# Edge marks written before the edge counts, edge maxima beside the projections, and four heads gathered in BF16 halves

## The chip, the cores and the metric

One Trainium2 chip, of which the kernel uses one core. The time is the device time of one launch in microseconds (us). Three runs of the kernel before gave 1710.49, 1711.12 and 1711.81 us: the median is 1711.12. A further execution was profiled, and all rows below come from it.

## The reference

A graph transformer layer on 1250 nodes of 768 features with 21250 edges. The layer norm of `x` feeds a graph attention network (GNN, three layers of four heads of 192 channels on the same 21250 edges) and a linear-attention mixing (12 heads of 64, 256 random features); both are added to `x`. After a second norm comes a mixture of 8 experts.

```python
def gat_conv(x, src, dst, W, a_src, a_dst, b):        # for each of the 3 layers, N=1250, H=4, C=192
    h = (x @ W).reshape(N, H, C)
    e = leaky_relu(((h * a_src).sum(-1))[src] + ((h * a_dst).sum(-1))[dst], 0.2)
    m = segment_max(e, dst, N)
    p = exp(e - m[dst])
    s = segment_sum(p, dst, N)
    out = segment_sum((p / (s[dst] + 1e-16))[:, :, None] * h[src], dst, N)
    return out.reshape(N, H * C) + b
x1 = relu(xn @ W_ah + b_ah)                           # xn = layernorm(x)
node = relu(concat([relu(gat_conv(x1, ...)) for 3 layers], 1) @ W_out + b_out)
# mixing: q, k, v = xn @ w_qkv.T
# q' = ratio * (exp(q.proj - diag - max over features) + eps), k' likewise with one maximum over all keys
# mix = (q' @ (k'.T @ v)) / (q' @ sum k') @ w_proj.T + b_proj
x = x + node + mix
x = x + ffn(layernorm(x))                             # top-1 switch to 8 experts, capacity 195
```

## The kernel before

The edges are turned into a dense table of counts: `count[s, d]` says how often edge s to d occurs (1250 x 1250). With it a GAT head is dense work: the weight of a pair is exp(leaky_relu(as[s] + ad[d]) - shift[d]) times its count, and the sum over edges is a matrix product of these weights with `h`. A head has ten *items*: half of the destinations (640 or 610) by a pair of source tiles (2 x 128). Twelve heads make 120 items. The nodes lie in 10 tiles of 128 (the last has 98), so `NT` is 10.

One item goes through four steps. `edge_z` on DVE (`L1538`, two instructions) adds the source term to the shifted destination rows `shift_b`; `edge_exp` on ACT (`L1931`, two) is the exponential; `weigh` on DVE (`L1547`, one of 1280 columns) takes the minimum with 1 and multiplies by the counts; `gather` on PE (`L1085`, ten FP32 matmuls of 193 columns, each shown as two by the trace) multiplies with the rows `hb`. Five buffers `eb` hold weights. After a half head, `evict` (ACT) and `finish` divide and store.

The shifts need, for each head and destination, the largest source term among its edges. `edge_max` on DVE (`L1503`) takes it over 1250 sources for one tile of destinations: 120 instructions. Its other operand, `absent`, is 0 at an edge and a very large negative number elsewhere; `shifts` then makes the head's shift, and SP writes it to memory and reads it back spread over the partitions (`shift_b`, in `head_in`).

How the counts come about: GpSimd (POOL) fills three tables in device memory with zeros (`table<-zero`), then adds 170 groups of 125 edges into them with indirect DMAs (`L2142`, `table<-amount,place`), each table's adds waiting for the last ones into the same table. `tab_in` reads ten tiles of each table back, DVE's `count_` sums the three, ACT copies to BF16 (`count16`), PE transposes them (`count_turn`, 100 of 128x128), and DVE makes `absent` of the transposed tile.

All engines follow one order of steps, written by generators (`whole_order`), and each engine runs its own steps of it in that order, held back only by semaphores. `first_order` holds the norm, `x1` = relu(...), and `h` of three layers. Then two streams are laced together: `projection_steps` (v products, `L912` and neighbours; q and k products of six pairs of heads; `k_top`, the maxima of the keys, whose banks `L1028` reuses) followed by `mix_steps`, and beside it `graph_steps`. In `mix_steps` each pair of heads has ten k steps (`dash`, `L1102`; `k_sum`, `L1117`) and ten q steps (`q_max`, `L1570`; `q_turn`; `q_out`, `L1145`, for two tiles), and then the rows: `row_turn` (`L1160`), `row_mm` (output products of 18 matmuls of 384 columns), 10 row tiles for the mixing and 10 for each GNN layer. A GNN layer's row tiles wait for that layer's 40 gathers. `graph_steps` waits for the count adds to be in (`COUNTS_AT`, q/k product 17), then does counts and `absent`, then edge maxima, then items. The rates (`COUNT_RATE`, `EDGE_RATE` and others) say how many steps of the second stream go by one of the first. In `features`, `warm_mix` issues two idle matmuls of 512 columns on PE with each step until the items are open.

After the rows comes the tail: norm, switch, experts, with the indirect reads `L2162` of 105 or 90 rows on POOL.

## Time and profile before

| what | value |
|---|---|
| runs | 1710.49, 1711.12, 1711.81 us |
| profiled execution | 1709.37 us, its span 1707.6 us |
| mean granted TensorE clock | 0.962 |
| busy share of the span | PE 90%, weight load 70%, DVE 67%, ACT 40%, POOL 24% |
| stages: norm, x1, h | to 311 us |
| v products; q and k products | 314 to 377; 377 to 571 |
| mixing without items; mixing with items | 571 to 646; 646 to 972 |
| items and row products | 972 to 1387 |
| last row products; tail | 1387 to 1431.5; 1431.5 to 1707.6 |

The span runs from the first to the last instruction, and the execution is 1.77 us longer. Row products of the first tile start at 1013.6 us. The page's 40 slices, of 42.7 us each:

```profile
PE   3989999999878789998999989998999999986987
PEld 2556666555444568988888988888888976656664
DVE  6677664105567989999987787668766833885323
ACT  3420001122233366877777763346434621441110
POOL 3688888888500000000000000000000000002331
PEclk9989999999989899999999999999999999986999
```

Each digit is a tenth of the slice (9 is 90% or more). POOL is busy with the count adds to slice 11. DVE is nearly idle in slice 8, where the v products run, and nearly full in slices 14 to 22, where edge maxima, mixing and items come together. PE is at 9 in nearly every slice after 30: from there on it is PE that is short.

### The profile page before, as it was taken

What the parts mean: (1) busy time and instruction counts of PE and PEld (TensorE: products, weight loads), DVE (VectorE), ACT (ScalarE), POOL (GpSimd) and SP (SyncE); (2) the same over time, 40 slices, a digit from 0 to 9 for tenths busy, and PEclk for the clock granted to TensorE, in tenths of its full rate; (3) what the DMA queues carried; (4) which work ended last, traced back from release to release, by engine and by line L of the source; (5) the groups of instructions that cost most, each with busy time, mean ns of one, the idle gap of its engine ahead of it and who ended that gap; (6) DMA issues with size and microseconds to landing.
All of it is one profiled execution on the core that took longest, in us unless ns stands there. A gap on an engine that the chain in (4) does not pass through costs nothing.

```text
span 1707.6 us, 25848 instructions
## 1 busy us (share of the span) xinstructions
PE 1541.5 (90%) x10083; PEld 1186.8 (70%) x10109; DVE 1149.2 (67%) x2629; ACT 681.4 (40%) x1359; POOL 410.1 (24%) x251
## 2 busy tenths in 40 slices
PE   3989999999878789998999989998999999986987
PEld 2556666555444568988888988888888976656664
DVE  6677664105567989999987787668766833885323
ACT  3420001122233366877777763346434621441110
POOL 3688888888500000000000000000000000002331
PEclk9989999999989899999999999999999999986999
DMA  9435545464752514324420354236413224545951
GB/s 342 97 64 113 111 84 122 71 93 75 190 187 87 143 42 120 88 90 114 125 71 28 104 166 162 96 126 197 129 38 103 82 68 153 213 181 203 319 158 50
DMA packets 196620, 213.72 MB, mean 125 GB/s; under 512 B 81551, under 2 KB 149789, under 8 KB 196498
## 3 DMA queue, kind: packets, MB, share of 16 engines
q1 hardware_dynamic: 119874, 187.01, 34.6%
q0 software_dynamic: 75760, 22.70, 8.8%
q10 hardware_dynamic: 864, 2.36, 0.4%
q8 instruction: 80, 1.31, 0.3%
q14 instruction: 42, 0.34, 0.1%
HBM read 144.74 MB, written 68.40 MB: 125 GB/s over the span
## 4 chain that ended last, share of the span: by engine, by line
PE 45%; DVE 19%; POOL 17%; DMA 9%; issue 7%; ACT 3%; SPq 1%; POOLq 0%; ACTq 0%; DVEq 0%
PE bank L1085 17%; POOL table L2142 17%; DVE junk L1503 5%; PE bank L913 4%; PE bank L911 4%; PE bank L912 4%; PE bank L1261 4%; DMA table<-amount,place 3%; PE bank L1249 3%; DVE eb L1538 2%; DVE eb L1547 2%; PE bank L1145 2%; DMA table<-zero 2%; PE bank L1117 1%; PE bank L1102 1%
## 5 line engine op out<-in xcount | busy, mean ns | idle before, releaser
L1085 PE MATMUL bank<-hb,eb 128*128 128x193 f32 (+3 forms) x2400 | 418.8, 332 | 14.5 <-ACT node L1945 9.2
L1085 PEld LDWEIGHTS bank<-hb,eb 128*128 128x128 f32 (+3 forms) x2400 | 399.5, 191 | 20.6 <-issue 10.5
L2142 POOL DMA_INDIRECT table<-amount,place x170 | 345.2, 2030 | 74.4 <-issue 49.1
L2148 POOL IOTA iota8i<- 128x8 int32 x1 | 0.1, 140 | 941.7 <-DMA node_rows<-node 941.7
L1538 DVE SCALAR_TENSOR_TENSOR eb<-shift_b,as_low,shift_b 128x640 f32<-128x640 f32 (+1 forms) x240 | 196.4, 860 | 0.3 <-PE bank L1085 0.2
L1931 ACT ACTIVATE eb<-eb,asd 128x640 f32<-128x640 f32 (+1 forms) x240 | 181.5, 812 | 28.9 <-DVE eb L1538 28.9
L1547 DVE SCALAR_TENSOR_TENSOR eb<-eb,count 128x1280 f32<-128x1280 f32 (+1 forms) x120 | 174.6, 1455 | 2.3 <-ACT eb L1931 2.3
L1503 DVE CUSTOM_DVE_ANT_0 junk<-ab,absent 128x1250 bf16<-128x1250 f32 x120 | 174.3, 1453 | 1.5
L911 PE MATMUL bank<-w_o_hi,aT_hi 128*128 128x384 bf16 (+1 forms) x360 | 119.1, 331 | 0.0
L911 PE MATMUL bank<-wg_hi,x1T_hi 128*128 128x384 bf16 (+3 forms) x360 | 118.9, 330 | 0.1
L913 PE MATMUL bank<-w_o_hi,aT_lo 128*128 128x384 bf16 (+1 forms) x360 | 119.0, 330 | 0.0
L912 PE MATMUL bank<-w_o_lo,aT_hi 128*128 128x384 bf16 (+1 forms) x360 | 118.9, 330 | 0.0
L912 PE MATMUL bank<-wg_lo,x1T_hi 128*128 128x384 bf16 (+3 forms) x360 | 118.8, 330 | 0.0
L913 PE MATMUL bank<-wg_hi,x1T_lo 128*128 128x384 bf16 (+3 forms) x360 | 118.8, 330 | 0.0
L912 PE MATMUL bank<-xnT_lo,wq_hi 128*128 128x512 bf16 (+1 forms) x212 | 74.9, 353 | 4.6 <-DVE wq_lo L1339 3.0
L1377 DVE TENSOR_TENSOR h_row<-bank,bgr 128x384 f32<-128x384 f32 (+1 forms) x60 | 32.5, 555 | 64.8 <-PE bank L913 64.7
L913 PE MATMUL bank<-xnT_hi,wq_lo 128*128 128x512 bf16 (+1 forms) x215 | 75.8, 352 | 0.2
L1803 DVE TENSOR_TENSOR orow<-bank,b2r 105x384 f32<-105x384 f32 (+1 forms) x32 | 17.8, 555 | 82.8 <-PE bank L1261 82.8
L1970 ACT ACTIVATE ef<-bank,q_shift 128x256 f32<-128x256 f32 (+1 forms) x120 | 50.5, 473 | 51.2 <-DVE q_shift L1575 51.0
L911 PE MATMUL bank<-xnT_hi,wq_hi 128*128 128x512 bf16 (+1 forms) x201 | 70.8, 352 | 0.1
L1877 ACT ACTIVATE wg_hi<-stage 128x776 bf16<-128x776 f32 x18 | 15.3, 850 | 135.5 <-DVE stage L1353 135.5
L1945 ACT ACTIVATE node<-bank 128x386 f32<-128x386 f32 (+1 forms) x72 | 29.3, 442 | 88.3 <-PE bank L1085 88.3
(280 smaller groups left out, 2965.9 us busy)
## 6 DMA issues: line engine op xcount, KB each, us to landing
w<-in_w SPq DMA_DIRECT2D x16, 1152.0 KB, 12.5
shift_b<-shift_rows SPq DMA_DIRECT2D x24, 625.0 KB, 5.8
h_rows<-h_row SPq DMA_DIRECT2D x27, 388.0 KB
hb<-h_rows SPq DMA_DIRECT2D x12, 873.0 KB
ar<-node_rows SPq DMA_DIRECT2D x27, 384.0 KB
table<-zero POOLq DMA_DIRECT2D x3, 3054.0 KB, 21.7
tab<-table SPq DMA_DIRECT2D x27, 312.5 KB, 3.6
qk_rows<-qk_row SPq DMA_DIRECT2D x12, 625.0 KB
```

The costliest lines, as they stand in the source:

```text
L911: T.matmul(out_ap, lhs[0], rhs[0], start=first, stop=False, skip_group_check=skip)
L912: T.matmul(out_ap, lhs[0], rhs[1], start=False, stop=False, skip_group_check=skip)
L913: return T.matmul(out_ap, lhs[1], rhs[0], start=False, stop=last, skip_group_check=skip)
L1085: ins = T.matmul(bank[w // 2][0:M, c0:c0 + GC + 1], p[0:K, u, w * P:w * P + M], hv[0:K, t, 0:GC + 1], start=opens and u == 0 and w % 2 == ...
L1249: ins = T.matmul(bank[i % 2][:, 0:CAP], w1s[e % WEIGHT_SETS][:, k, f * 128:(f + 1) * 128], sT_of(k)[:, e * CAP:(e + 1) * CAP], start=k == ...
L1261: ins = T.matmul(bank[4 + i % 4][0:r1 - r0, 0:HROWS], hT[e % 2][:, f, r0:r1], w2s[e % WEIGHT_SETS][:, f, cs], start=f == 0, stop=f == KF - 1)
L1503: V.tensor_tensor_reduce(out=junk[0:R, :], in0=ab[lh % 2][0:R, :], in1=absent[0:R, t, :], scale=1.0, scalar=-BIG, op0=ALU.add, op1=ALU.max ...
L1538: ins = V.scalar_tensor_tensor(eb[i % EDGE_BUFFERS][:, u, 0:w], low, as_low[:, t, lh:lh + 1], high, ALU.add, ALU.max)
L1547: V.scalar_tensor_tensor(e, e, 1.0, count[:, 2 * pair:2 * pair + 2, ns], ALU.min, ALU.mult).then_inc(sem["edge_w"], 1)
L1931: ins = A.activation(e[:, u, 0:w], e[:, u, 0:w], ACT.Exp, bias=asd[:, t, 8 * l + hh:8 * l + hh + 1])
L1970: ins = A.activation(ef[g % 4][0:R, hh, :], bank[3 + g % 2][0:R, hh * FEATS:(hh + 1) * FEATS], ACT.Exp, bias=bias)
L2142: G.indirect_dma_start(tables[i], bass.IndirectOffsetOnAxis(place[:, c:c + 1], axis=0), amount16[:, c:c + 1], None, compute_op=ALU.add).th ...
```

## The change

**Marks.** Three new tables in device memory, `marks`, in BF16, are filled with the large negative number, and 0 is written at each edge, at the transposed place, and at the whole diagonal (one DMA of 1250 elements). These 170 indirect DMAs write and don't add (`L2191`). They stand on POOL where the 170 adds stood. SP reads ten tiles of each into `absent` and two `tab` buffers (`absent_in`), and DVE takes the maximum of the three (two instructions a tile, `absent_`). `count_turn` and `count16` are gone.

**Counts.** The 170 adds stand on POOL behind the marks (`scatter`), and `tab_in` stands behind them, on POOL too and no longer on SP. The zero fills of the three count tables stand among the marks, at groups 4, 5 and 6 of `place`. In the order, counts come at step 78 of the mixing (`COUNTS_AT`), the first items behind them.

**Edge maxima.** Five stand beside the v products, 30 beside the q and k products, two at the maximum of the keys, then 0.9 for each mixing step; 107 stand ahead of `tab_in` and 13 behind it.

**Halves.** For heads 8 to 11 (the third layer, items 80 to 119) `h` is stored as two BF16 halves in the room of one FP32 number, and the weights are split in place: their high half is the upper 16 bits, and `weigh_lo` on DVE (`L1419`, 1280 columns) writes the rest, rounded, into the lower. `gather` is then 30 BF16 matmuls of 193 columns for ten FP32 ones. Both operands have a stride of two elements. In `h` of that layer ACT writes the high halves and DVE the low ones.

**Order.** `warm_mix` is gone from the mixing steps. The rates change. The last mixing step stands beside item 39 (before: 48), the first GNN row tile beside item 51 (54), row tile 10 beside item 99 (85), row tile 20 behind all items (112).

```diff
-COUNTS_AT = 17
-COUNT_RATE, EARLY_EDGE_RATE, FIRST_EDGE_RATE, EDGE_RATE, ATTENTION_RATE = 0.5, 0.75, 1.1, (1.1, 0.5), (0.4, 0.5)
+MARKS_AT, COUNTS_AT = 6, 78
+COUNT_RATE, VALUE_EDGE_RATE, KEY_EDGE_RATE, MIX_EDGE_RATE, ATTENTION_RATE = 1.0, 1.8, 0.4, 0.9, (0.8, 0.77)
+SPLIT_FROM = 8
...
     yield from paced((key_steps(), 1), (tiles, 1), (first_nodes(), 1))
+    for q in range(PIECES):
+        yield "scatter", q
...
 def graph_steps(done):
-    while "scattered" not in done:
+    yield "ab_in", 0
+    for _ in range(MARKS_AT):
         yield None
-    yield "ab_in", 0
-    yield from paced((in_step([(3, lambda t: [("count_turn", t), ("absent", t)]), (1, lambda t: [("count", t)]),
-                               (0, lambda t: [("tab_in", t)])], NT), COUNT_RATE))
+    yield from in_step([(1, lambda t: [("absent", t)]), (0, lambda t: [("absent_in", t)])], NT)
     edges = edge_steps(done)
...
+    while "counts" not in done:
+        yield None
+    yield from paced((in_step([(1, lambda t: [("count", t)]), (0, lambda t: [("tab_in", t)])], NT), COUNT_RATE))
     yield "head_in", 0
...
-        if "open" not in done:
-            yield "warm_mix", 2
+        if n == COUNTS_AT:
+            done.add("counts")
...
@@ gather, PE @@
+                        for n, (p_part, h_part) in enumerate(((0, 0), (0, 1), (1, 0))):
+                            ins = T.matmul(bank[w // 2][0:M, c0:c0 + GC + 1],
+                                           eb_parts[i % EDGE_BUFFERS][p_part][0:K, u, w * P:w * P + M],
+                                           hb_parts[lh % 2][h_part][0:K, t, 0:GC + 1], start=begins and n == 0,
+                                           stop=ends and u == 1 and n == 2, skip_group_check=True)
@@ absent_, DVE @@
+                V.tensor_tensor(absent[0:R, t, :], absent[0:R, t, :], others[0], ALU.max).then_inc(sem["absent_first"], 1)
+                ve.wait_ge("absent_first", t + 1)
+                V.tensor_tensor(absent[0:R, t, :], absent[0:R, t, :], others[1], ALU.max).then_inc(sem["absent_done"], 1)
@@ weigh_lo, DVE @@
+                ve.wait_ge("weighed", i - ITEMS * SPLIT_FROM + 1)
+                V.tensor_tensor(low, eb[i % EDGE_BUFFERS][:, :, 0:w], high, ALU.subtract).then_inc(sem["edge_w"], 1)
@@ place_, POOL @@
                 if q == 0:
+                    ge.wait_ge("marks_set", 32)
+                    G.dma_start(marks[2].rearrange("(p t n) o -> p t (n o)", p=P, n=MARKS[1]),
+                                fill[:, :].unsqueeze(1).broadcast_to([P, MARKS[0], MARKS[1]])
+                                ).then_inc(sem["table_zero"], 16)
+                    G.dma_start(marks[0][0:N * (N + 1), :].rearrange("(p r s) o -> p r (s o)", p=EP, s=N + 1)[:, :, 0:1],
+                                none[0:EP, 0:N // EP].unsqueeze(2), allow_slow_non_contiguous=True
+                                ).then_inc(sem["marks_set"], 16)
+                if 4 <= q < 4 + TABLES:
+                    G.dma_start(tables[q - 4].rearrange("(p t n) o -> p t (n o)", p=P, n=TABLE[1]),
...
+                                    [P, TABLE[0], TABLE[1]])).then_inc(sem["table_zero"], 16)
+                ge.wait_ge("placed", 2 * q + 1)
                 for c in range(q * CP, min((q + 1) * CP, CHUNKS)):
                     i = table_of(c)
+                    if i == 0:
+                        ge.wait_ge("marks_set", 48)
                     if i == 2:
+                        ge.wait_ge("table_zero", 16)
+                    ge.wait_ge(f"marked{i}", 16 * added(c, i))
+                    G.indirect_dma_start(marks[i], bass.IndirectOffsetOnAxis(mark_at[:, c:c + 1], axis=0),
+                                         none[0:EP, 0:1], None).then_inc(sem[f"marked{i}"], 16)
@@ tab_in, now POOL @@
+                for i in range(TABLES):
+                    ge.wait_ge(f"scatter{i}", 16 * added(CHUNKS, i))
+                ge.wait_ge("counted", TABLES * (t - 1))
@@ absent_in, SP @@
+                for i in range(TABLES):
+                    sy.wait_ge(f"marked{i}", 16 * added(CHUNKS, i))
+                sy.wait_ge("absent_done", t - 1)
```

POOL's instructions from the marks or adds on, in the kernel before (`L2142` are the adds):

```order
L2122 MEMSET h_row_229 128x4
L2132 DMA table<-zero 1024x1x1527
L2142 DMA table<-amount_72,place 1563648x1 x170
L2148 IOTA iota8i 128x8
L2149 IOTA idx_i 128x10
```

and after (`L2191` the marks, `L2213` the adds, `L2203` the reads of `tab_in`):

```order
L2173 DMA marks<-fill 1024x1x1528
L2176 DMA marks<-zero 1250x1x1
L2191 DMA marks<-zero,mark_at 1564672x1 x32
L2180 DMA table<-zero 1024x1x1527
L2191 DMA marks<-zero,mark_at 1564672x1 x8
L2180 DMA table<-zero 1024x1x1527
L2191 DMA marks<-zero,mark_at 1564672x1 x8
L2180 DMA table<-zero 1024x1x1527
L2191 DMA marks<-zero,mark_at 1564672x1 x122
L2213 DMA table<-amount_72,place 1563648x1 x170
L2203 DMA tab_148<-table 128x1250
```

One chain of adds has become a chain of marks with three fills in it, and the adds and the reads of the tables follow it on the same engine.

DVE among items and the splitting of output weights (`w_o_lo`, `L1590`), in the kernel before:

```order
L1547 SCALAR_TENSOR_TENSOR eb_157<-eb_157,count 128x2x610
L1590 TENSOR_TENSOR w_o_lo<-st_0_242,w_o_hi 128x768
L1590 TENSOR_TENSOR w_o_lo<-st_1_243,w_o_hi 128x768
L1538 SCALAR_TENSOR_TENSOR eb_155<-shift_b_251,as_low,shift_b_250 128x640 x2
L1547 SCALAR_TENSOR_TENSOR eb_153<-eb_153,count 128x1280
L1590 TENSOR_TENSOR w_o_lo<-st_0_242,w_o_hi 128x768
L1590 TENSOR_TENSOR w_o_lo<-st_1_243,w_o_hi 128x768
L1538 SCALAR_TENSOR_TENSOR eb_156<-shift_b_251,as_low,shift_b_250 128x640 x2
L1547 SCALAR_TENSOR_TENSOR eb_154<-eb_154,count 128x1280
```

and after, in the heads in halves (`L1573` is `edge_z`, `L1582` is `weigh`, `L1419` is `weigh_lo`, `L1625` splits output weights):

```order
L1573 SCALAR_TENSOR_TENSOR eb_157<-shift_b_229,as_low,shift_b_228 128x640 x2
L1419 TENSOR_TENSOR eb_160<-eb_160 128x2x610
L1625 TENSOR_TENSOR w_o_lo<-st_1_246,w_o_hi 128x768
L1582 SCALAR_TENSOR_TENSOR eb_156<-eb_156,count 128x1280
L1573 SCALAR_TENSOR_TENSOR eb_158<-shift_b_229,as_low,shift_b_228 128x640 x2
L1419 TENSOR_TENSOR eb_156<-eb_156 128x1280
L1625 TENSOR_TENSOR w_o_lo<-st_0_245,w_o_hi 128x768
L1625 TENSOR_TENSOR w_o_lo<-st_1_246,w_o_hi 128x768
L1582 SCALAR_TENSOR_TENSOR eb_157<-eb_157,count 128x1280
```

Each item has one more instruction of 1280 columns, between its `weigh` and its gather, and up to two splits stand with it as before.

PE at the first steps of the mixing, before (`L1046` are the idle matmuls):

```order
L1046 MATMUL bank<-ident_61 128x512 x2
L1102 MATMUL bank<-feats_hi,k_first 128x256
L1102 MATMUL bank<-feats_lo,k_first 128x256
L1102 MATMUL bank<-feats_hi,k_first 128x256
L1102 MATMUL bank<-feats_lo,k_first 128x256
L1117 MATMUL bank<-v_first,ef_212 128x65 x4
L1046 MATMUL bank<-ident_61 128x512 x2
```

and after (`L1116` is `dash`, `L1131` is `k_sum`):

```order
L1116 MATMUL bank<-feats_hi,k_first 128x256
L1116 MATMUL bank<-feats_lo,k_first 128x256
L1116 MATMUL bank<-feats_hi,k_first 128x256
L1116 MATMUL bank<-feats_lo,k_first 128x256
L1131 MATMUL bank<-v_first,ef_215 128x65 x4
L1116 MATMUL bank<-feats_hi,k_first 128x256
```

The two idle matmuls of each step are gone, and up to the counts nothing stands between the mixing's own matmuls.

## Rows read from the trace of the kernel before

**Rows 1.** Busy time of each engine by stretch of the span; its second row names the columns.
```profile
core 0: us, PE busy (x) PEld busy (x) DVE busy (x) ACT busy (x) POOL busy (x), PEclk, DMA share, GB/s
314.00:377.00 63.00, 60.04 (x362) 36.66 (x362) 2.33 (x11) 11.09 (x22) 54.57 (x28) 0.98 0.51 74
377.00:571.00 194.00, 162.42 (x1327) 92.52 (x1345) 126.24 (x242) 52.72 (x93) 64.84 (x32) 0.93 0.48 127
571.00:646.00 75.00, 65.37 (x433) 48.07 (x432) 67.39 (x128) 47.60 (x105) 0.00 (x0) 0.90 0.43 115
646.00:972.00 326.00, 300.26 (x2205) 287.51 (x2203) 289.01 (x480) 241.56 (x535) 0.00 (x0) 0.98 0.31 88
972.00:1387.00 415.00, 405.23 (x2507) 352.32 (x2506) 300.21 (x394) 191.91 (x346) 0.00 (x0) 0.99 0.37 120
1387.00:1431.50 44.50, 44.50 (x288) 29.36 (x287) 14.82 (x35) 7.84 (x19) 0.96 (x6) 1.00 0.24 72
1431.50:1707.60 276.10, 230.06 (x1338) 166.70 (x1335) 146.30 (x398) 64.60 (x139) 47.64 (x48) 0.91 0.58 193
```

**Rows 2.** Timeline of POOL, indirect adds: start us, busy us, what, [idle before it <-releaser].
```profile
48.80 2.12 POOL L2142 DMA_INDIRECT table<-amount,place  x1 [13.02 <-DMA table<-zero]
...
57.22 1.99 POOL L2142 DMA_INDIRECT table<-amount,place  x1 [3.98 <-DMA table<-amount,place]
...
453.36 1.99 POOL L2142 DMA_INDIRECT table<-amount,place  x1 [0.30 <-issue]
```

**Rows 3.** DMA issues of the page: count, KB each, us from issue to landing.
```profile
shift_b<-shift_rows SPq DMA_DIRECT2D x24, 625.0 KB, 5.8
...
table<-zero POOLq DMA_DIRECT2D x3, 3054.0 KB, 21.7
...
tab<-table SPq DMA_DIRECT2D x27, 312.5 KB, 3.6
```

**Rows 4.** Source view of L2162: ns min/median/max, first and last start.
```profile
L2162 POOL DMA_INDIRECT sr<-xf_rows,from_row x16: 956/986/1542, 1554.7 to 1644.9; - x16
```

**Rows 5.** Timeline of DVE in the mixing, before the first gather.
```profile
602.15 0.69 DVE L1570 TENSOR_REDUCE q_max<-bank 128x2 f32<-128x512 f32 x1
...
604.32 0.69 DVE L1570 TENSOR_REDUCE q_max<-bank 128x2 f32<-128x512 f32 x1
```

**Rows 6.** Timeline of DVE, one item of edge weights and one edge maximum.
```profile
640.41 1.68 DVE L1538 SCALAR_TENSOR_TENSOR eb<-shift_b,as_low,shift_b 128x640 f32<-128x640 f32 x2
642.00 1.48 DVE L1547 SCALAR_TENSOR_TENSOR eb<-eb,count 128x1280 f32<-128x1280 f32 x1
643.40 1.46 DVE L1503 CUSTOM_DVE_ANT_0 junk<-ab,absent 128x1250 bf16<-128x1250 f32 x1
```

**Rows 7.** Groups of instructions by form: xcount, busy us, mean ns of one, idle before.
```profile
L1431 DVE TENSOR_TENSOR sq<-sq 128x512 bf16<-128x512 f32 x24 | 17.6, 735 | 27.6 <-ACT sq L1911 27.6
...
L1339 DVE TENSOR_TENSOR wq_lo<-stage,wq_hi 128x768 bf16<-128x768 f32 x12 | 11.5, 959 | 63.1 <-ACT wq_hi L1867 63.1
```

**Rows 8.** Timeline of PE: mixing, row products, a gather.
```profile
590.29 0.27 PE L1102 MATMUL bank<-feats_hi,k_first 128*128 128x256 bf16 x1
...
590.73 1.01 PE L1117 MATMUL bank<-v_first,ef 128*128 128x65 f32 x8
...
609.67 1.90 PE L1145 MATMUL bank<-context,qf 128*128 128x65 f32 x16
...
1204.15 3.43 PE L1085 MATMUL bank<-hb,eb 128*128 128x193 f32 x20
...
1386.78 0.82 PE L1160 MATMUL bank<-ident,ar 128*128 128x128 f32 x6
...
1399.79 0.82 PE L1160 MATMUL bank<-ident,ar 128*128 128x128 f32 x6
```

**Rows 9.** Waits of PE from 392 to 572 us: us in total, times, longest.
```profile
PE bank L1028 <- DVE kmax L1454: 14.6, 12, 3.8
```

More of the change, by code:

```diff
@@ L238, in product @@
         n, c = divmod(m, NC)
-        if m == COUNTS_AT:
-            done.add("scattered")
+        if m == 0:
+            done.add("products")
         if c == 0 and n + 2 < 2 * PAIRS:
@@ L319, in edge_z, with split_weigh, weigh_last @@
         yield "edge_z", i
+    def split_weigh(i):
+        if i // ITEMS >= SPLIT_FROM:
+            yield "weigh", i
+    def weigh_last(i):
+        yield "weigh_lo" if i // ITEMS >= SPLIT_FROM else "weigh", i
     def of_half(name):
@@ L334, in mark @@
         return []
[L336 to L338 removed]
+    yield from in_step([(5, of_half("finish")), (5, mark), (4, of_half("evict")), (2, split_weigh), (0, edge_z),
+                        (1, lambda i: [("edge_exp", i)]), (2, weigh_last), (3, lambda i: [("gather", i)])],
+                       LH * ITEMS)
     yield "expert_setup", 0
@@ L565, in program @@
         tables = [dram(f"table{i}", (P * TABLE[0] * TABLE[1], 1), U16) for i in range(TABLES)]
+        marks = [dram(f"marks{i}", (P * MARKS[0] * MARKS[1], 1), BF16) for i in range(TABLES)]
         h_rows = dram("h_rows", (LAYERS, N, GH, HW))
@@ L685, in program @@
         tab = [[put(f"tab{i}{j}", [P, N], U16) for j in range(2 + i)] for i in range(2)]
-        count16 = [put(f"count16_{i}", [P, N], BF16) for i in range(2)]
         assert cursor[0] <= r_d
```

195 lines of the change are left out of this document (107 added, 88 removed), and 2 rows, old and new, of the table TAKEN_OVER.

## The prediction, on record before the kernel ran

> **What bounds the kernel now.** I read the table of engines first, then the slices, then the busy time by stretch, and then for each stretch the view that names its limit. In the stretches PE has 162.4 of 194 us beside the q and k products, 300.3 of 326 with mixing and items, 405.2 of 415 with items and row products, 44.5 of 44.5 behind the last gather, while DVE has 2.3 of 63 us beside the v products and 67.4 of 75 in the mixing that has no items yet [rows 1]. So from the first gather at 646 on PE is the limit (with DVE close behind to 972), and ahead of it there is a stretch of 75 us in which DVE makes edge maxima and the mixing must keep step with it. The counts decide when that may begin: POOL adds from 48.8 to 453.36 us, 2.29 us from one to the next where nothing disturbs it (1.99 + 0.30 idle) and 396/167 = 2.37 on the average from 57.22 on [rows 2]. In the waits, PE stands 14.6 us for the key maxima on DVE in the q and k products [rows 9], because DVE has counts, `absent` and the first edge maxima there.
>
> The total of the profiled execution is 1709.37, which is 1.77 above its span and 1.75 below the median of the runs. I work on the span and add both.
>
> **The change part by part.**
>
> *Marks.* The row nearest to an indirect DMA that writes and doesn't add is the tail's: 986 ns, against 1990 ns for an add [rows 2, 4]. With the 0.30 us between, 1.3 us a mark. That row reads 3 KB a line, and a mark writes 2 bytes at 125 places as the adds do, so the two ends are 1.3 and 2.3 us; I take 1.3, since what doubles the add's time is most likely the adding. The first add started at 48.8, when two fills were in [rows 2]; the third marks fill now waits for these, some 9 us, and the diagonal another 3: first mark at 62. 170 x 1.3 = 221, and three zero fills among them hold each the queue behind them for about 9 us (three fills at once take 21.7 to land [rows 3]): 27. Marks are in at about 310. The steps that read them stand at the seventh v product of 20, 314 + 1.5 + 7 x 2.95 = 336. So SP isn't held. `absent` is then 20 maxima of BF16 on DVE, which is idle there.
>
> *Projections.* The v products: 60 of 63 us are PE's own [rows 1]; I add 1.5 for the wait at start: q/k begin at 378. These took 194 us with 162.4 of PE work, of which about 6 are the removed transposes. Left are 156 plus stalls. DVE had 126.2 there; counts and `absent` go (about 27), and 30 edge maxima of 1.5 us replace the fewer of before: about 135 us, under PE's. I put 8 us of stalls in place of 32: 164, ending at 542. Top of the keys to 549.
>
> *Mixing without items.* A q step has a pitch of 2.17 us with one edge maximum [rows 5], a k step a bit less. Of each pair's 20 steps ten cost 2.17 + 0.6 (since 12 maxima come with ten q steps) and ten 1.7: 43.5. Three pairs and ten k steps (17): the engines come to the counts at 549 + 147.5 = 697.
>
> *POOL's chain of adds.* 310 + 170 x 2.37 = 712.5, landing at 715. That is later than 697, so it is POOL that sets the counts. If marks or fills take less, at most 18 us come back. `tab_in` comes on POOL with two buffers: 3.6 us to land [rows 3], three DVE sums of about 0.8 and 0.8 and 0.15 a tile, two tiles per 7.7 us: ten tiles 42, at 757. The head's tables land 5.8 later [rows 3], then `edge_z`, exponential and `weigh`: first gather at **769**, 123 after the 646 of before. Between 549 and 697 nothing is lost by this but place: 70 mixing steps are done that stood beside items before.
>
> *After the first gather.* I sum by the order, taking in each section the engine with the most work. A FP32 gather is 20 passes in 3.27 us, a row product 13.01/4 = 3.25 us, from the two turns at 1386.78 and 1399.79, a k step 0.44 + 0.90, a q step 0.44 + 0.44 + 0.90 (half of the 1.9 for two tiles, less its end) [rows 8].
> 1. Gathers 0 to 38 with 17 k and 20 q steps: 127.5 + 22.8 + 35.6 = 186 us, PE.
> 2. Gathers 39 to 79 with 18 row products: 134 + 58.5, and 3 us where DVE is late: 196 us, PE.
> 3. Gathers 80 to 119, in halves. On PE the same columns in three BF16 passes for two [rows 8]: if each runs at its 193 columns in half of a FP32 pass (0.082 for 0.1635 us), a gather is 2.46 for 3.27, and 40 save 33 us. On DVE an item is `edge_z` 1.59, `weigh` 1.40 to 1.48 [rows 6], and `weigh_lo`. For this, FP32 in and BF16 out, 512 columns take 735 and 768 take 959 ns [rows 7]: 224 per 256 more, so 1280 columns give 1.41 long; with weights of 1220, and a stride of two that no row shows, 1.4. Its ends are 0.85 (at half the rate) and 1.8. So 4.4 us, 4.55 with finish. The first 21 (to item 100) have six splits of output weights (0.9) and two row products beside them: DVE 21 x 4.55 + 5.4 = 101, PE 58: DVE. The last 19 have 14 row products: PE 46.7 + 45.5 = 92, DVE 19 x 4.55 and 14 x 1.3 for row halves = 104: DVE by little. Together 205 us.
> 4. 26 row products without items: 84.5, PE.
>
> The sum is 186 + 196 + 205 + 84.5 = 671.5. The same count of before's order gives 777 from the first gather to row tile 30, and the trace has 1431.5 - 646 = 785.5 [rows 1], 8.5 more. So I add 8: 679.5, 106 less than before. Of these 106, 70 steps of mixing moved ahead, and 33 come from PE's halves, of which DVE takes most back.
>
> *Cut elsewhere.* The 60 idle matmuls (78 less 18; 13 us of PE) lay in time where PE waited, in 571 to 646: nothing by themselves. `h` of layer three costs DVE about 1.1 us a tile more, beside PE's h products, which are longer: nothing. The tail stays 276.1 [rows 1].
>
> Total: 769 + 679.5 + 276.1 = 1724.6 of span; + 1.77 + 1.75 = **1728**; I write 1729 for rounding of the parts. It is 18 us slower than before: 123 late at the first gather against 106 back.
>
> **What a rule says against it.** The row shows FP32 matmuls of 193 columns at 0.1635 us a pass with whole numbers in a row; no row of this stage has a moving operand with gaps. The Trainium skill (SBUF — State Buffer, "Door 1: The DMA port swizzle", the note on cachelines) says that reads lose speed only when fewer than two hits fall in a 16-byte line, and lets BF16 be strided to 8 elements. By that rule a stride of two runs at full rate, as I took; without it rival D would hold.
>
> The granted clock was 0.90 in 571 to 646, with the idle matmuls in it, and 0.98 and 0.99 behind [rows 1]. The Trainium skill (TensorE: Matmul & The Clock Gate, Part 1) has the clock follow how busy the array has lately been. By it the mixing without idle matmuls may fall to the low level of 1.2 GHz; what that would do here is rival C.
>
> **The rivals.**
> - *B, DVE doesn't bind in the halves, and POOL or DVE are ahead elsewhere: faster.* If `weigh_lo` costs 0.85 or less, an item is 3.9 on DVE and section 3 becomes PE's or near it: 205 falls to some 165 (-40). If the zero fills don't hold the marks and the adds keep to 2.29, 15 to 18 us come back at the counts. Both give 1729 - 55 = **1674**. For it: rows of half-width output at 0.87 ns a column [rows 7] are not DVE's quickest form. Against: input is still FP32.
> - *C, the clock falls in the mixing without items.* Between 549 and 697 PE has 1.34 to 1.78 us of work in steps of 1.7 to 2.8, and at 1.2 GHz that becomes 2.7 to 3.6: PE sets the pace, 70 steps x 3.1 = 217 for 147. That ends at 766 for 697, 51 behind POOL's 715, less what one tick of overlap gives back: + 41, **1770**. For it: 0.90 there already [rows 1]. Against: PE stays at more than half of its time.
> - *D, a strided moving operand at half rate.* Each of 1200 BF16 matmuls takes 0.163 instead of 0.082: a gather 4.9, 40 x 4.9 + 52 of row products = 248 for 205, and a few more where both alternate: + 48, **1777**.
> - *E, a mark costs what an add costs.* 62 + 170 x 2.3 + 27 = 480 for the marks, SP stands at `absent_in` from 336 and with it the loads of q and k weights, and the adds end at 885: **1890**. It decides once a mark takes over about 1.45 us (310 would pass 336).
>
> **How the numbers follow.** The forecast has 0.50, B 0.22, C 0.12, D 0.08, E 0.06, something else 0.02. The forecast's own range is 1705 to 1750: 18 us below for POOL's part, 20 above for DVE stalls in the projections. A measurement of this kernel can tell 0.2%, 3.4 us, from no change. Faster: B and a tenth or two of the forecast's own, 0.30; within 0.2%: 0.07; slower: 0.63. The range takes in B and C: 1680 to 1775.
>
> **What would show it.** Right: marks on POOL 1.3 us apart, the last at about 310; the last add at about 712; first gather at about 769; DVE without gaps in gathers 80 to 100 at about 4.5 us an item, PE with gaps there; 30 matmuls of a gather in 2.5 us; row tile 30 at about 1449. Wrong: marks beyond 336 (E); a granted clock near 0.5 between 549 and 769 (C); a gather in halves of 4.9 us (D); or the first gather before 745 with items of 3.9 us (B).

## The result, and the profile after

Four runs of the changed kernel gave 1838.15 to 1846.45 us, median 1839.38, against 1710.8 for the kernel before: a ratio of 1.0765, 95% interval 1.0732 to 1.0799. The forecast was 1729 with a range of 1680 to 1775. The direction was right, the size was not: 129 us slower instead of 18. One execution of the kernel of experiment 7 was disturbed (3077.8 us where the others of that kernel took 1839 to 1848) and is left out of its times.

The profiled execution took 1846.45 us, its span 1844.7. It is the slowest of the four, 7 us above the median, and all rows of the changed kernel come from it. The stretches of the changed kernel, cut at its own events (v products, mixing without items, the gap, items in FP32, items in halves, last row products, tail):

```profile
core 0: us, PE busy (x) PEld busy (x) DVE busy (x) ACT busy (x) POOL busy (x), PEclk, DMA share, GB/s
312.00:407.00 95.00, 65.96 (x364) 38.56 (x364) 15.89 (x31) 8.70 (x19) 66.42 (x47) 0.84 0.58 137
589.00:766.00 177.00, 151.51 (x959) 132.03 (x957) 130.88 (x255) 118.05 (x274) 147.49 (x66) 0.76 0.49 82
766.00:881.00 115.00, 38.98 (x182) 32.88 (x182) 36.66 (x68) 24.06 (x61) 64.83 (x55) 0.52 0.41 106
881.00:1273.00 392.00, 383.77 (x2527) 359.20 (x2526) 313.07 (x430) 239.10 (x470) 0.00 (x0) 0.99 0.35 109
1273.00:1469.00 196.00, 158.56 (x1495) 137.46 (x1493) 191.85 (x210) 92.00 (x163) 0.00 (x0) 0.97 0.31 103
1469.00:1563.00 94.00, 92.11 (x586) 60.40 (x584) 33.83 (x68) 17.88 (x39) 0.96 (x6) 0.98 0.30 88
1563.00:1844.70 281.70, 232.85 (x1338) 168.92 (x1336) 146.41 (x398) 64.77 (x139) 47.55 (x48) 0.91 0.57 189
```

The row that matters is the third: for 115 us PE is busy for 39, DVE for 37, ACT for 24. All of them have come to the counts, and the counts are not there: up to 824 POOL still adds, and from there it reads the tables. The first gather starts at 881.3 instead of 646 [rows 1], 235 us later. Behind it the kernel is quicker than before: 681.8 us to row tile 30, where before took 785.5. The tail has 281.6 for 276.1. 235 - 104 + 5.5 = 137, the difference of the two spans.

What POOL does meanwhile, from its timeline (start, busy us, what, idle before it):

```profile
59.85 1.28 POOL L2191 DMA_INDIRECT marks<-zero,mark_at  x1 [12.68 <-DMA marks<-zero]
...
64.44 1.19 POOL L2191 DMA_INDIRECT marks<-zero,mark_at  x1 [0.30 <-issue]
...
111.26 0.96 POOL L2180 DMA_DIRECT2D table<-zero  x1
...
128.01 1.19 POOL L2191 DMA_INDIRECT marks<-zero,mark_at  x1 [11.11 <-DMA marks<-zero,mark_at]
...
364.88 1.19 POOL L2191 DMA_INDIRECT marks<-zero,mark_at  x1 [0.30 <-issue]
366.38 2.03 POOL L2213 DMA_INDIRECT table<-amount,place  x1 [0.30 <-issue]
...
819.97 1.99 POOL L2213 DMA_INDIRECT table<-amount,place  x1 [0.31 <-issue]
824.23 2.29 POOL L2203 DMA_DIRECT2D tab<-table  x4 [2.27 <-DMA table<-amount,place]
```

From 60 to 824 POOL issues marks, fills and adds, or waits between them. An undisturbed mark takes 1.19 + 0.30 = 1.49 us. Behind each fill a few marks still go out, then POOL waits for one to land: 11.1, 10.7 and 9.4 us. The chain of adds begins when the last mark is out, and `tab_in` when the last add has landed. POOL's groups by form (xcount, busy us, mean ns, idle before them):

```profile
L2213 POOL DMA_INDIRECT table<-amount,place x170 | 372.8, 2193 | 83.1 <-issue 46.0 <-DMA table<-amount,place 37.0
L2191 POOL DMA_INDIRECT marks<-zero,mark_at x170 | 211.1, 1242 | 104.9 <-issue 46.7 <-DMA marks<-zero,mark_at 44.9 <-DMA marks<-zero 12.7
```

The adds of the kernel before:

```profile
L2142 POOL DMA_INDIRECT table<-amount,place x170 | 345.2, 2030 | 74.4 <-issue 49.1 <-DMA table<-zero 13.0 <-DMA table<-amount,place 12.3
```

An add has become longer: 2193 ns on the average for 2030, and the waits for landings are 37.0 us for 12.3. In both kernels the adds are the same 170 instructions.

Last, the halves. DVE's groups by form, and the first two gathers in halves on PE:

```profile
L1573 DVE SCALAR_TENSOR_TENSOR eb<-shift_b,as_low,shift_b 128x640 f32<-128x640 f32 x120 | 100.6, 881 | 5.0 <-PE bank L1093 4.9
...
L1582 DVE SCALAR_TENSOR_TENSOR eb<-eb,count 128x1280 f32<-128x1280 f32 x60 | 89.2, 1487 | 4.4 <-ACT eb L1972 4.4
...
L1419 DVE TENSOR_TENSOR eb<-eb 128x1280 bf16<-128x1280 f32 x20 | 33.5, 1677 | 0.0
L1419 DVE TENSOR_TENSOR eb<-eb 128x1220 bf16<-128x1220 f32 x20 | 31.9, 1596 | 0.1
```

```profile
1273.00 5.39 PE L1097 MATMUL bank<-hb,eb 128*128 128x193 bf16 x60
1278.24 0.32 PE L930 MATMUL bank<-w_o_hi,mix_aT_hi 128*98 128x384 bf16 x1
```

60 BF16 matmuls follow each other in 5.24 us, 0.087 each, against 0.1635 for an FP32 pass [rows 8]. That is 7% above half of it, so the strided operands run near full rate, and rival D (0.163) is out. But `weigh_lo` costs 1.64 us, and in the stretch of the halves DVE is busy for 191.9 of 196 us, PE for 158.6. PE waits there 34.8 us for it:

```profile
PE bank L1097 <- DVE eb L1419: 34.8, 20, 3.0
```

### The profile page after: what moved, and what is told of

The parts are those of the page before. It is cut to its first block, busy times and chain, and to the rows that moved or that the text cites. A ratio compares the mean times of both kernels' runs of the same rounds, so it can differ in the third digit from the quotient of the medians.

```text
span 1844.7 us, 26649 instructions
## 1 busy us (share of the span) xinstructions
PE 1551.1 (84%) x10349; PEld 1187.8 (64%) x10349; DVE 1226.0 (66%) x2705; ACT 683.8 (37%) x1369; POOL 669.9 (36%) x455
## 4 chain that ended last, share of the span: by engine, by line
PE 34%; POOL 23%; DVE 18%; DMA 15%; issue 7%; ACT 2%; SPq 0%; POOLq 0%; DVEq 0%; ACTq 0%
POOL table L2213 16%; PE bank L1093 12%; POOL marks L2191 7%; DMA table<-amount,place 6%; DMA marks<-zero,mark_at 5%; DVE eb L1573 4%; PE bank L930 4%; PE bank L931 4%; PE bank L932 4%; PE bank L1275 3%; DVE eb L1582 3%; PE bank L1263 3%; DVE eb L1419 3%; DMA tab<-table 1%; PE bank L1174 1%
## 5 line engine op out<-in xcount | busy, mean ns | idle before, releaser
L2213 POOL DMA_INDIRECT table<-amount,place x170 | 372.8, 2193 | 83.1 <-issue 46.0
L1093 PE MATMUL bank<-hb,eb 128*128 128x193 f32 (+3 forms) x1600 | 274.7, 329 | 8.0 <-DVE eb L1582 6.0
L1093 PEld LDWEIGHTS bank<-hb,eb 128*128 128x128 f32 (+3 forms) x1600 | 263.3, 189 | 11.1 <-DVE eb L1582 7.2
L2191 POOL DMA_INDIRECT marks<-zero,mark_at x170 | 211.1, 1242 | 104.9 <-issue 46.7
L1573 DVE SCALAR_TENSOR_TENSOR eb<-shift_b,as_low,shift_b 128x640 f32<-128x640 f32 (+1 forms) x240 | 197.3, 866 | 9.3 <-PE bank L1093 9.2
L1582 DVE SCALAR_TENSOR_TENSOR eb<-eb,count 128x1280 f32<-128x1280 f32 (+1 forms) x120 | 174.7, 1455 | 4.4 <-ACT eb L1972 4.4
L1097 PE MATMUL bank<-hb,eb 128*128 128x193 bf16 (+3 forms) x1200 | 115.6, 255 | 37.4 <-DVE eb L1419 34.8
L1097 PEld LDWEIGHTS bank<-hb,eb 128*128 128x128 bf16 (+3 forms) x1200 | 108.1, 102 | 44.9 <-DVE eb L1419 42.0
L1144 PE MATMUL bank<-ident,ef 128*128 128x128 f32 (+1 forms) x240 | 43.6, 313 | 90.9 <-ACT ef L2011 90.6
L1144 PEld LDWEIGHTS bank<-ident,ef 128*128 128x128 f32 (+1 forms) x240 | 31.8, 164 | 100.1 <-ACT ef L2011 99.1
L2233 POOL DMA_INDIRECT sr<-xf_rows,from_row x16 | 16.6, 1034 | 217.7 <-DVE to_row L1812 212.8
```

The lines of the kernel that those rows point to most:

```text
L1093: ins = T.matmul(bank[w // 2][0:M, c0:c0 + GC + 1], p[0:K, u, w * P:w * P + M], hv[0:K, t, 0:GC + 1], start=begins, stop=ends and u == 1, ...
L1097: ins = T.matmul(bank[w // 2][0:M, c0:c0 + GC + 1], eb_parts[i % EDGE_BUFFERS][p_part][0:K, u, w * P:w * P + M], hb_parts[lh % 2][h_part][ ...
L1144: ins = T.transpose(bank[5 + q % 2][:, k * P:k * P + R], ef[g % 4][0:R, hh, m * 128:(m + 1) * 128], ident_of(t))
L1573: ins = V.scalar_tensor_tensor(eb[i % EDGE_BUFFERS][:, u, 0:w], low, as_low[:, t, lh:lh + 1], high, ALU.add, ALU.max)
L1582: V.scalar_tensor_tensor(e, e, 1.0, count[:, 2 * pair:2 * pair + 2, ns], ALU.min, ALU.mult).then_inc(sem["weighed" if lh >= SPLIT_FROM els ...
L2191: G.indirect_dma_start(marks[i], bass.IndirectOffsetOnAxis(mark_at[:, c:c + 1], axis=0), none[0:EP, 0:1], None).then_inc(sem[f"marked{i}"] ...
```

## The experiments

The theory at the start: POOL's chain of 170 marks and 170 adds sets the first gather, and DVE sets the pace in the halves. The rivals: the mixing without items is late by itself (its clock), the halves do save PE's time, and traffic rather than DVE stretches the adds. In each text on record "before" is the unchanged kernel.

### 1. The changed kernel without halves (no_halves)

```diff
-SPLIT_FROM = 8
+SPLIT_FROM = 12
```

> The changed kernel with heads 8 to 11 in FP32 again; everything else stays. The chain theory (POOL's marks and adds set the first gather, DVE sets the pace in the halves): first gather stays near 881 us; items 80 to 119 become PE's, 40 x 3.27 + 16 x 3.25 = 183 us for the 196 of the changed kernel, so about 1826 us (-13). The rival (the halves save PE's 33 us as they stand) expects 196 + 33, about 1872 us.

Measured: 1825.08 us (1820.15 to 1830.10), 14 below the changed kernel. The first gather is at 875.1; items 80 to 119 take 181 us (1267 to 1448) for 196:

```profile
1267.00:1448.00 181.00, 177.14 (x1094) 160.66 (x1093) 134.87 (x170) 90.86 (x160) 0.00 (x0) 1.00 0.34 111
```

PE is busy for 177 of 181 us: the stretch is PE's again, and shorter. The halves cost 14 us in this order. The rival is out. (The text on record counts 16 row products in this stretch; the trace has 14, 84 of the matmuls of one line at six a product.)

### 2. A fifth of the adds (few_adds)

```diff
-MARKS_AT, COUNTS_AT = 6, 78
+MARKS_AT, COUNTS_AT, ADDS = 6, 78, 34
...
@@ tab_in, POOL @@
-                    ge.wait_ge(f"scatter{i}", 16 * added(CHUNKS, i))
+                    ge.wait_ge(f"scatter{i}", 16 * added(ADDS, i))
@@ scatter, POOL @@
-                for c in range(q * CP, min((q + 1) * CP, CHUNKS)):
+                for c in range(q * CP, min((q + 1) * CP, ADDS)):
```

> The changed kernel with 34 of the 170 adds into the count tables; the other 136 are left out, so the counts are incomplete. The chain theory: the last add is at about 460 us, the other engines come to the counts at about 766 as before, first gather about 766 + 57 = 823, so about 1782 us (-58). The rival (the mixing without items and idle matmuls is what is late, at its low clock, and POOL only waits along): first gather stays near 881, 1839 us.

Measured: 1769.09 us (1763.64 to 1775.26), 70 less. The last add is at 458.5 and the engines reach the counts at 755, about as in the changed kernel (765); the first gather is at 805.0. So POOL's chain decides, by 70 us, and no more than that: the other engines come late as well, and the kernel is still 3.6% slower than the one before (ratio 1.0363, 1.0328 to 1.0397).

### 3. Short edge maxima (short_max)

```diff
-MARKS_AT, COUNTS_AT = 6, 78
+MARKS_AT, COUNTS_AT, WD = 6, 78, 50
...
@@ edge_max, DVE @@
-                V.tensor_tensor_reduce(out=junk[0:R, :], in0=ab[lh % 2][0:R, :], in1=absent[0:R, t, :],
+                V.tensor_tensor_reduce(out=junk[0:R, 0:WD], in0=ab[lh % 2][0:R, 0:WD], in1=ab[lh % 2][0:R, 0:WD],
```

> The changed kernel with each edge maximum over 50 columns instead of 1250, so that the maxima are not those of the edges. If DVE's edge maxima are what stretches POOL's adds (2.19 us for 1.99): adds of about 2.03 us, the chain of adds 29 us shorter, about 1810 us. The rival (traffic in the DMA queues holds the adds' landings, and DVE has no part in it): adds stay at 2.19 and the time within 5 us of 1839, since POOL still comes last.

Measured: 1812.09 us (1808.15 to 1815.34), 27 less. POOL's groups in this kernel:

```profile
L2213 POOL DMA_INDIRECT table<-amount,place x170 | 345.0, 2029 | 85.8 <-issue 44.5 <-DMA table<-amount,place 41.3
L2191 POOL DMA_INDIRECT marks<-zero,mark_at x170 | 211.6, 1245 | 99.7 <-issue 44.2 <-DMA marks<-zero,mark_at 40.1 <-DMA marks<-zero 12.3
```

The adds are back at 2029 ns, 170 x 164 ns = 28 us, which is the whole difference; the waits for landings stay (41.3 for 37.0). So both causes are there, and they part cleanly: DVE's edge maxima beside the adds stretch POOL's own instruction, and the landings are held by something else. The mixing's 70 steps change as well:

```profile
577.00:713.00 136.00, 118.98 (x952) 102.57 (x950) 44.44 (x251) 115.73 (x273) 106.86 (x54) 0.96 0.58 105
```

They take 136 us for 176, with DVE busy for 44 of them, and the granted clock is 0.96 for 0.76 though no idle matmul was put back. Experiments 5 and 6 come back to this.

### 4. Only the halves, on the kernel before (halves_only)

The diff is the part of the change on halves, put into the kernel before: `SPLIT_FROM = 8`, the split `h` of layer three, `weigh_lo`, and the three BF16 matmuls.

```diff
+        yield "weigh_lo" if i // ITEMS >= SPLIT_FROM else "weigh", i
```

> The kernel before with only the halves of heads 8 to 11 put in; marks, counts, edge maxima and the order stay as before. The theory that DVE sets the pace in the halves: items 80 to 119 take on DVE 40 x 4.4 + 26 x 1.3 + 11 = 221 us for the 218 of before, so about 1715 us. The rival (PE's 33 us are saved, DVE's addition is hidden): about 1678 us.

Measured: 1706.39 us (1702.39 to 1711.31), ratio 0.9981 (0.9965 to 0.9997). Neither number: nearly nothing is gained, but nothing lost. Items 80 to 119 take 215 us for 218, with DVE busy for 209 of 216, PE for 198. The kernel before, and this one:

```profile
1168.00:1387.00 219.00, 218.61 (x1355) 189.59 (x1356) 152.40 (x203) 99.67 (x182) 0.00 (x0) 0.99 0.30 98
1172.00:1388.00 216.00, 197.52 (x1755) 164.30 (x1756) 208.71 (x243) 100.07 (x183) 0.00 (x0) 0.97 0.31 99
```

So the stretch passes from PE to DVE at nearly no gain: PE's busy time falls by 21 us (by the 0.087 of a matmul, 40 x (3.27 - 2.62) = 26), and DVE gets 40 x 1.64 = 66 more. Here 26 row products stand beside the items, in the changed kernel 14. PE without the halves would need 40 x 3.27 + 26 x 3.25 = 215 here and 176 there, DVE with them was busy for 209 and 192; by these sums the halves cost 14 us there and nothing here.

### 5. A fifth of the marks and of the adds (few_both)

The edit of experiment 2, and:

```diff
@@ place_, POOL @@
-                for c in range(q * CP, min((q + 1) * CP, CHUNKS)):
+                for c in range(q * CP, min((q + 1) * CP, ADDS)):
@@ absent_in, SP @@
-                    sy.wait_ge(f"marked{i}", 16 * added(CHUNKS, i))
+                    sy.wait_ge(f"marked{i}", 16 * added(ADDS, i))
@@ edge_max, DVE @@
-                V.tensor_tensor_reduce(out=junk[0:R, :], in0=ab[lh % 2][0:R, :], in1=absent[0:R, t, :],
+                V.tensor_tensor_reduce(out=junk[0:R, :], in0=ab[lh % 2][0:R, :], in1=ab[lh % 2][0:R, :],
```

> The changed kernel with 34 of 170 marks and 34 of 170 adds, and edge maxima of the same size that read the source terms twice instead of the marks; so marks, counts and shifts are not the reference's. It asks what the order alone is worth once POOL is free. Theory: of the 60 us by which the kernel with few adds is slower than before, 40 come from SP, which stands at the reads of the marks until 360 us: q and k products start at 378 instead of 417, first gather at 765 instead of 805, about 1729 us, still 20 above the kernel before. The rival (the q and k products are late by the reads of the marks themselves, or by the clock): about 1769 us as with few adds.

Measured: 1743.21 us (1739.45 to 1748.31), 26 below few_adds. The q and k products start at 391.0 instead of 417.5, and the first gather is at 784.1. The direction is right. In the changed kernel PE waits here for two things:

```profile
PE bank L930 <- ACT v_row L1947: 28.7, 3, 23.5
PE bank L930 <- DVE wq_lo L1359: 16.0, 1, 16.0
```

The first is for ACT, which empties the banks of the v products into `v_row`, whose buffers SP stores between its reads of the marks; it falls to 0.9 us with few marks. The second, for the split of the first q and k weights, stays at 18.0, and with it 13 us of the delay; in the kernel before it is 3.0. What makes it long was not taken apart. The 70 steps without items take 175 us (559 to 734) though POOL is free:

```profile
559.00:734.00 175.00, 148.53 (x950) 129.92 (x948) 132.98 (x258) 116.89 (x272) 1.59 (x3) 0.77 0.33 88
```

PE is busy for 148.5 us at a mean granted clock of 0.77. That is about half of the time at the low level of 1.2 GHz, and with DVE at 133 of 175 this run doesn't tell which of the two holds the other.

### 6. The same with idle matmuls in the mixing (few_both_warm)

```diff
+        if n < COUNTS_AT:
+            yield "warm_mix", 2
```

> The kernel with few marks and few adds, with two idle matmuls of 512 columns in each mixing step up to the counts, as the kernel before has them. In the 70 steps without items it had PE busy 148.5 of 175 us at a granted clock of 0.77 and DVE 133. If that clock is what makes the mixing long (the clock theory): clock near 0.95, the 70 steps in about 150 us, total about 1720 us. If DVE's edge maxima set the pace: 175 us again, 1743 us.

Measured: 1726.66 us (1725.33 to 1732.30), 17 less. The 70 steps take 159 us (557 to 716), and the clock is up:

```profile
559.00:716.00 157.00, 144.77 (x1098) 113.87 (x1099) 130.57 (x256) 117.64 (x273) 1.59 (x3) 0.99 0.36 94
```

So the idle matmuls that the change took out were worth about 16 us in this stretch once POOL is out of the way. They are not the whole of it: with short edge maxima (experiment 3) the same steps took 136 us at a clock of 0.96 without any idle matmul. So it takes the full maxima on DVE and the missing idle matmuls together to bring the clock down to 0.77. Putting the idle matmuls back gives 16 us of the stretch, shortening the maxima 40, the clock included. In the changed kernel itself that loss lies under POOL's chain: its 70 steps too have a clock of 0.76 (the second of the stretches shown first), and end 55 us before the last add. The Trainium skill (TensorE: Matmul & The Clock Gate, Part 1) has the clock follow how busy the array has been; the two rows, 0.77 without and 0.99 with idle matmuls, agree.

### 7. The zero fills behind the marks (fills_late, fills_late_b)

```diff
@@ place_, POOL @@
-                if 4 <= q < 4 + TABLES:
-                    G.dma_start(tables[q - 4].rearrange("(p t n) o -> p t (n o)", p=P, n=TABLE[1]),
...
@@ scatter, POOL @@
+                if q == 0:
+                    for table in tables:
+                        G.dma_start(table.rearrange("(p t n) o -> p t (n o)", p=P, n=TABLE[1]),
...
```

> The changed kernel with the three zero fills of the count tables behind the last mark instead of among the marks. If the fills are what holds the marks (three waits of about 10 us): the last mark at about 334 us for 365, the first add some 20 behind it at 355 for 366, about 1828 us (-11). The rival (a mark's own 1.24 us and DVE's work beside it make the 1.80 us pace): the last mark stays near 360 and the fills come on top, about 1855 us.

Measured: 1846.18 us (1842.00 to 1847.82), ratio 1.0772 (1.0754 to 1.0790) where the changed kernel has 1.0765. The total doesn't say where the time went, so the same kernel was profiled once more:

> The kernel with the three zero fills behind the marks once more, for an undisturbed profile: total 1844 us as in its four undisturbed runs. By the total alone it stays open whether the marks end earlier and the fills cost the same behind them: then the last mark is at about 335 and the first add at about 372; or the marks end near 360 and the adds begin at 380.

Measured: 1840.57 us (1839.06 to 1842.01). POOL's timeline at the end of the marks:

```profile
334.56 1.18 POOL L2187 DMA_INDIRECT marks<-zero,mark_at  x1 [0.30 <-issue]
335.74 2.77 POOL L2206 DMA_DIRECT2D table<-zero  x3
371.60 2.10 POOL L2214 DMA_INDIRECT table<-amount,place  x1 [33.09 <-DMA table<-zero]
```

The last mark is at 334.6 for 364.9: the three fills had held the marks for 30 us, as the prediction had it (27), and the marks' waits for landings are 12.6 us where they were 44.9. But behind the marks the fills hold the adds for 33. My 1828 had 20 us for them there; it is all given back. And the q and k products start at 418 though the marks are out at 335. So the marks' own end is not what starts them. The reads of the marks now run beside the fills, and the first of them are slow: SP issues the third tile's read at 353.7 and the fourth's only at 374.9, when the fills are in; from there on it issues two tiles in some 8 us. PE's wait for `v_row`, whose stores stand among these reads in SP's order, stays at 22.4 us. That the fills are what slows the reads follows from these times alone; no run shows it by itself.

### 8. weigh_lo on POOL (pool_lo_8, pool_lo_4)

The diff is against the kernel of experiment 4; pool_lo_4 also has `SPLIT_FROM = 4`.

```diff
@@ weigh_lo, now POOL @@
-                ve.wait_ge("weighed", i - ITEMS * SPLIT_FROM + 1)
-                V.tensor_tensor(low, eb[i % EDGE_BUFFERS][:, :, 0:w], high, ALU.subtract).then_inc(sem["edge_w"], 1)
+                ge.wait_ge("weighed", i - ITEMS * SPLIT_FROM + 1)
+                G.tensor_tensor(low, eb[i % EDGE_BUFFERS][:, :, 0:w], high, ALU.subtract).then_inc(sem["edge_w"], 1)
```

> The kernel before with the halves of heads 8 to 11, and weigh_lo on POOL instead of DVE. 1640 ns for 768 columns on POOL make 2.7 us for 1280, under an item's 5.4 us. If DVE's addition is what eats the gain of the halves: items 80 to 119 take 215 - 33 = 182 us, about 1676 us. The rival (POOL's instruction and DVE's stretch each other, or its latency leaves PE without weights): about 1706 us as with the halves alone, or more.

> As the kernel before it in this list, with the halves in heads 4 to 11 (80 items). By the sums of PE and DVE for each ten items another 23 us over the 33: about 1653 us. The rival: items 40 to 79 are bound by DVE, whose instructions POOL stretches, and nothing more comes back: 1676 us or above.

Measured: 1723.68 us (1722.89 to 1726.00) for heads 8 to 11, 1750.78 (1749.30 to 1754.63) for heads 4 to 11: slower than before by 0.65% and 2.2% (ratios 1.0065, 1.0048 to 1.0082, and 1.0217, 1.0200 to 1.0234). The 1676 and 1653 are out, and four more heads in halves cost another 27 us. DVE's timeline of pool_lo_8, and POOL's of the same microseconds:

```profile
1229.82 3.73 DVE L1578 SCALAR_TENSOR_TENSOR eb<-shift_b,as_low,shift_b 128x640 f32<-128x640 f32 x2
...
1235.20 1.47 DVE L1587 SCALAR_TENSOR_TENSOR eb<-eb,count 128x1280 f32<-128x1280 f32 x1
1236.59 3.74 DVE L1578 SCALAR_TENSOR_TENSOR eb<-shift_b,as_low,shift_b 128x640 f32<-128x640 f32 x2
```

```profile
1229.97 2.90 POOL L2201 TENSOR_TENSOR eb<-eb 128x1280 bf16<-128x1280 f32 x1 [3.55 <-DVE eb L1587]
1236.75 2.90 POOL L2201 TENSOR_TENSOR eb<-eb 128x1280 bf16<-128x1280 f32 x1 [3.88 <-DVE eb L1587]
```

POOL begins when `weigh` has ended, which is when DVE begins its next `edge_z`. That pair takes 3.73 us for the 1.68 that it has alone [rows 6], two microseconds more; over the whole stretch one of its two instructions takes 1865 ns on the average, and 870 in experiment 4. DVE has given away an instruction of 1.64 us and lost 2.05. `weigh` itself, which runs when POOL has finished, stays at 1.47. The Trainium skill (GPSIMD Engine Reference, 1. Specifications) says that GpSimd shares its SBUF interfaces with VectorE and that they collide when a DVE instruction has two SBUF inputs, as `edge_z` does; the two timelines agree. The edge maxima of experiment 3 have two such inputs too.

### 9. Rounded weights (round_w, round_w_4)

The diff is against the kernel of experiment 4, with `weigh_lo` left out of the order; round_w_4 also has `SPLIT_FROM = 4`.

```diff
@@ weigh, DVE @@
+                o = eb_parts[i % EDGE_BUFFERS][0][:, :, 0:ns.stop - ns.start] if lh >= SPLIT_FROM else e
-                V.scalar_tensor_tensor(e, e, 1.0, count[:, 2 * pair:2 * pair + 2, ns], ALU.min,
+                V.scalar_tensor_tensor(o, e, 1.0, count[:, 2 * pair:2 * pair + 2, ns], ALU.min,
@@ gather, PE @@
-                        for n, (p_part, h_part) in enumerate(((0, 0), (0, 1), (1, 0))):
+                        for n, (p_part, h_part) in enumerate(((0, 0), (0, 1))):
```

> The kernel before with halves in heads 8 to 11, but the weights are only rounded to BF16 by weigh itself: the product with the weights' low half is left out, and weigh_lo with it. A gather is 20 BF16 matmuls (1.64 us for 3.27), DVE has nothing added. If DVE's 1.64 us for weigh_lo is what eats the gain of the halves: items 80 to 119 take about 172 us for 215 (DVE 40 x 3.15 + 26 x 1.3 + 11), total about 1668 us. If the strided operands or the loads of weights hold PE: 1700 us or more.

> As the kernel before with rounded weights, in heads 4 to 11 (80 items). By the sums of each ten items, items 40 to 79 go from PE's 208 us to DVE's 172 or so: about 1630 us. The rival: items 40 to 49 stand beside mixing and the rest is held by DVE more than the sum says, so little comes: 1655 us.

Measured: 1664.37 us (1662.22 to 1667.52), ratio 0.9716 (0.9693 to 0.9740); and 1637.52 (1631.04 to 1639.89), ratio 0.9556 (0.9527 to 0.9585). The stretch of items 80 to 119 in round_w:

```profile
1168.00:1343.00 175.00, 161.28 (x1353) 128.06 (x1354) 155.77 (x203) 98.56 (x181) 0.00 (x0) 0.97 0.39 122
```

175 us for 218 in the kernel before and 215 in experiment 4. Two things are gone at once: `weigh_lo` on DVE and a third of PE's matmuls (PE is busy for 161 us, and for 198 in experiment 4). So the run shows that strided halves can pay, and not what leaving out `weigh_lo` alone would bring; with three products PE's 198 us would be the floor. Both kernels beat the one before and the changed one, at the price of weights with 8 bits of mantissa in those heads. Two rows of the same kernel show what the new output costs DVE:

```profile
L1594 DVE SCALAR_TENSOR_TENSOR eb<-eb,count 128x1280 f32<-128x1280 f32 x40 | 59.4, 1484 | 0.0
...
L1594 DVE SCALAR_TENSOR_TENSOR eb<-eb,count 128x1280 bf16<-128x1280 f32 x20 | 33.1, 1656 | 0.0
```

The same operation that writes BF16 with a gap after each element takes 1656 ns for the 1484 that it takes to write whole FP32. It seems to be the gap and not the BF16: without gaps a `TENSOR_TENSOR` of 768 columns takes 949 ns with BF16 output and 951 with FP32 in the changed kernel.

## Why the prediction was wrong

**POOL decides the first gather: right, and the size of its chain is the step that failed:** the terms "170 x 1.3" for the marks and "170 x 2.37" for the adds. Of the 112 us by which the first gather came later than predicted (881 for 769), 109 lie in these two terms; some 6 belong to the profiled execution, for in experiment 1, with the same order up to there, the first gather was at 875.1.

- *"170 x 1.3 = 221" for the marks.* It was 305 (59.9 to 364.9). I took the price of a mark from an indirect read of 105 rows, 0.986 [rows 4]. A mark takes 1.19 undisturbed and 1.24 on the average: with 46.7 us of issue 258 us for 221, so 37 more. Waits for landings were 44.9 us where I had 27, 31.2 of them behind the three fills; the small ones, 13 us, were not in the sum at all. The fills' own 3 us are the rest. It was 55 us late at the end. The prediction had the two ends, 1.3 and 2.3, and a point at 1.45 from which SP would be held: the mark came out at 1.49 alone and 1.80 with its waits, and SP was held. That part of rival E came true. Its price of a mark (2.3) did not, and its total of 1890 was 51 us too high where mine was 110 too low.
- *"170 x 2.37" for the adds.* It was 458 from the first add to the reads (366.4 to 824.2) for 405. 2.37 is the mean of the kernel before, and in that kernel not one edge maximum stood beside the adds: the first starts at 545.1, the last add at 453.4. The change puts 107 of them there, and experiment 3 measures these: 28 us, 0.26 for each. The other 25 are waits for landings, 37.0 us for 12.3; 16.8 of them lie between 366 and 415, when 9 MB of marks are read. That these reads cause them was not tested by itself. I moved an instruction beside another and kept its old price.

**The other engines at the counts by 697: wrong by 68, and hidden.** They came at 765. The q and k products took 160 us against 164 predicted, but started at 422.8 instead of 378; the mixing took 176 for 147.5. The first is in large part the hold of SP at the marks (experiment 5: 26 us of the total), the second in part the clock (experiment 6: 16 us with idle matmuls) and in part DVE's edge maxima (experiment 3: 40 us with short ones, the clock included). Rival C, "the clock falls in the mixing without items", was half right: 0.76 was granted there. But PE didn't set the pace at 217 us; the steps took 176, with PE busy for 151. And POOL came later still. The low level reads off from single matmuls in the changed kernel:

```profile
763.10 0.42 PE L1116 MATMUL bank<-feats_lo,kT 128*98 128x256 bf16 x1
763.31 0.42 PE L1116 MATMUL bank<-feats_hi,kT 128*98 128x256 bf16 x1
763.52 0.42 PE L1116 MATMUL bank<-feats_lo,kT 128*98 128x256 bf16 x1
```

They follow each other in 0.21 us, where four take 0.44 at full clock [rows 8].

**`tab_in` on POOL, 54 us to the first gather: right,** 57.

**After the first gather, 679.5: right,** 681.8. The sections were 190, 202, 196 and 94 for 186, 196, 205 and 84.5, 10.5 more in sum, and the 8 added from the kernel before covered most of it. In the halves `weigh_lo` was 1.64 on the average and 1.68 for 1280 columns, not 1.41. A strided output costs `weigh` 11% (experiment 9), which no row before showed and which would make 1.57; the rest is open. The section was shorter even so, because DVE had up to four items begun before the first gather in halves, and because 14 row products stood in it and not 16. The last section had 28 for the 26 predicted. That the total came out within 3 us is in part luck. "DVE takes most back" was too mild: with 14 row products beside them the halves lose 14 us (experiment 1).

**"The 60 idle matmuls: nothing by themselves": true of the sum, not of the stretch.** In the changed kernel they would be hidden under POOL, whose last add comes 55 us after the mixing. Without that cover they are worth about 16 us.

**The tail** took 5.5 us more; 4 of these are in row tiles 30 to 39. That was not followed up.

**Three slips in the working.** By its own terms a pair's 20 steps make 44.7 us and not 43.5. The sum for rival E makes 1899, not 1890. And the range of 1680 to 1775 is said to take in B, whose time is 1674. None of them touches the result.

Where the 129 us are: 70 in the adds (experiment 2), 26 in the marks (5), 17 in the clock of the mixing (6), which makes 1726.7. Less the 14 of the halves (1), measured in another combination, that would be about 1713, the kernel before. This last step is arithmetic and no run. By the ratios to the kernel before, measured anew beside each group of kernels, the four steps are 69, 33, 13 and 13 us. So a single step is known to some 7 us, and their sum better (127 and 128).

## What to carry to other kernels

A chain on one queue engine is priced by its own instruction in its own new surroundings, not by the mean of its old ones. What stands beside it counts: here DVE's edge maxima added 28 us to a chain of 170 adds on POOL, and a POOL instruction added 2 us to DVE's work on every item. And when work goes from one engine to another to relieve the first, sum both over the stretch where it lands: three BF16 passes for two FP32 ones saved some 26 us of PE and cost 66 of DVE, and the only faster version was the one with neither the cost on DVE nor the third pass.
